# Row numbers kept as integers beside the rows, padding rows that name spare rows themselves, and no limiting operation per tile

## What is computed

```python
logits = x @ Wg + bg                                   # 8 experts
topk_vals, topk_idx = top_k(logits, 2)
topk_w = softmax(topk_vals)
h  = relu(x @ W1[e] + b1[e])                           # 256 -> 512, for each chosen expert e
eo = h @ W2[e] + b2[e]                                 # 512 -> 256
y  = x + sum over the 2 chosen experts of topk_w * eo
out = gamma * (y - mean(y)) * rsqrt(var(y) + 1e-5) + beta
```

## Time and profile before

| | us |
|---|---|
| median of 3 runs | 2370.67 (2370.27 to 2372.32) |
| profiled execution, its own time | 2372.47 |
| profiled execution, span of its instructions | 2370.8 |
| TensorE busy | 2167.7 (91%) |
| VectorE busy | 2049.7 (86%) |
| GpSimd busy | 1875.7 (79%) |
| ScalarE busy | 1661.8 (70%) |

### The profile page before, as it was taken

How to read it: one execution, slowest core, us unless ns; L and a number is a source line. 1 busy time by engine, 2 the same in 40 slices (tenths; PEclk the granted TensorE clock), 3 DMA queues, 4 the chain that set the end, 5 groups by cost and what they waited for, 6 DMA issues and landing times. The chain is left out here.

```text
span 2370.8 us, 47215 instructions
## 1 busy us (share of the span) xinstructions
PE 2167.7 (91%) x13383; PEld 1744.9 (74%) x13384; DVE 2049.7 (86%) x2983; ACT 1661.8 (70%) x3402; POOL 1875.7 (79%) x1176
## 2 busy tenths in 40 slices
PE   8889899999989898989899999999878999989995
PEld 5667677776767777767677777677677989979884
DVE  5899999999999999999999999999997556647775
ACT  6686878878787878776878877777774444436553
POOL 3787989898898989888889898988896566556563
PEclk9999999999999999999999999999998999999998
DMA  5041313223241404131314233231425667657674
GB/s 176 1 144 46 134 60 129 86 94 109 72 146 44 160 21 162 44 136 51 129 55 134 72 108 100 81 121 59 132 65 189 112 129 148 113 81 130 138 142 110
DMA packets 213919, 246.71 MB, mean 104 GB/s; under 512 B 96723, under 2 KB 178675, under 8 KB 213556
## 3 DMA queue, kind: packets, MB, share of 16 engines
q1 hardware_dynamic: 163092, 191.29, 26.2%
q0 software_dynamic: 29904, 34.77, 8.2%
q10 hardware_dynamic: 20688, 17.85, 2.5%
HBM read 180.50 MB, written 63.32 MB: 103 GB/s over the span
## 5 line engine op out<-in xcount | busy, mean ns | idle before, releaser
L878 POOL TENSOR_TENSOR dbu<-drive_u,w_all 128x1024 f32<-128x1024 f32 x384 | 904.2, 2363 | 102.0 <-DVE ps_a L742 49.2
L1157 ACT ACTIVATE ps_a<-delta,a_neg 128x512 f32<-128x512 f32 x768 | 517.3, 685 | 141.3 <-DVE area L742 124.8
L895 POOL TENSOR_TENSOR wp<-area 128x1024 f32<-128x1024 f32 x192 | 453.0, 2359 | 36.5 <-DVE area L742 35.8
L2024 POOL DMA_INDIRECT acc_scratch<-ow,idx x135 | 220.0, 1630 | 208.8 <-DMA acc_scratch<-ow,idx 127.4
L754 DVE TENSOR_TENSOR wd<-ps_a,area 128x1024 f32<-128x1024 f32 x320 | 383.9, 1200 | 0.0
L1421 PEld LDWEIGHTS ps_y<-ident,wd 128*128 128x128 f32 x2560 | 304.0, 145 | 97.3 <-issue 71.4
L1421 PE MATMUL ps_y<-ident,wd 128*128 128x128 f32 x2560 | 342.0, 279 | 10.7 <-DVE wd L754 10.5
L1448 PEld LDWEIGHTS ps_a<-dg,duT 128*128 128x128 f32 x2048 | 253.0, 199 | 66.6 <-issue 64.3
L1448 PE MATMUL ps_a<-dg,duT 128*128 128x128 f32 x2048 | 263.4, 284 | 38.2 <-ACT carry L1164 35.7
L2235 PEld LDWEIGHTS e_ps_h<-xT,w_tile 128*128 128x128 f32 x2160 | 261.7, 193 | 25.7 <-DVE xT L1913 14.0
L2235 PE MATMUL e_ps_h<-xT,w_tile 128*128 128x128 f32 x2160 | 266.5, 277 | 12.8 <-DVE xT L1913 8.1
(11 more groups left out here) (252 smaller groups left out, 3762.5 us busy)
## 6 DMA issues: line engine op xcount, KB each, us to landing
area<-b_scratch SPq DMA_DIRECT2D x128, 512.0 KB, 4.7
w_all<-b_scratch SPq DMA_DIRECT2D x96, 512.0 KB, 4.1
dg<-xs_scratch SPq DMA_DIRECT2D x540, 32.0 KB
area<-in_L_attn_x_dram SPq DMA_DIRECT2D x32, 512.0 KB, 5.0
x_scratch<-area SPq DMA_DIRECT2D x16, 512.0 KB, 2.9
acc_scratch<-area SPq DMA_DIRECT2D x16, 512.0 KB
area<-x_scratch ACTq DMA_DIRECT2D x32, 256.0 KB
ee<-acc_scratch SPq DMA_DIRECT2D x32, 256.0 KB, 3.3
```

The costliest lines, as they stand in the source:

```text
L878: pool.tensor_tensor(dbu[:, k % NBU], du[:, g % 2, :].unsqueeze(1).broadcast_to([P, 2, CH]), bb[:, row:row + 2, :], ALU.mult).then_inc(dbu ...
L895: pool.tensor_tensor(wp[:, s % 2], ss[:, s % 2], cc[:, rows, :], ALU.mult).then_inc(wp_done, 1)
L1157: act.activation(dst, dl[:, g, :], ACT.Exp, scale=a_neg[:, g, n:n + 1]).then_inc(exp_done, 1)
L2024: pool.indirect_dma_start(out=acc_dram, out_offset=bass.IndirectOffsetOnAxis(ap=idx[:, old, :], axis=0), in_=ow[:, old, :], in_offset=None ...
```

## The change

Row numbers are written into column 257 as integers: the two ScalarE copies write to the same bytes seen as int32. The padding buffer becomes `pads`, four copies (RING) of 128 rows, and its column 257 holds the integer numbers of spare rows, T*P + 128*k + p, written by GpSimd in the place of `aside`. `store_pad` and `tail_store` take the copies in turn. `idx`, `aside` and their semaphores go; the scatter takes its indices straight from column 1 of `meta[:, slot]`, seen as uint32. So that a slot of `meta` is not overwritten while its scatter may still read it, the load of tile s now waits for `t_out[slot]`, the landing of the scatter of tile s-4, where it waited for `o_weighed` and `idx_done`.

```diff
 row_meta (mamba_block), and "columns1" likewise
-                act.copy(stage[:, :, D + 1], idf[:, 0, q * NT:(q + 1) * NT]).then_inc(meta, 1)
+                act.copy(stage[:, :, D + 1].bitcast(I32), idf[:, 0, q * NT:(q + 1) * NT]).then_inc(meta, 1)
 moe_block
-        pad = sb("pad", [P, D + 2])
+        pads = sb("pads", [P, RING, D + 2])
-        aside = sb("aside", [P, RING])
-        idx = sb("idx", [P, RING, 1], U32)
 tail_store, store_pad
-                    sync.dma_start(xs_dram[r:r + P, :], pad[:]).then_inc(pad_out, 16)
+                    sync.dma_start(xs_dram[r:r + P, :], pads[:, j % RING]).then_inc(pad_out, 16)
-                    sync.dma_start(acc_dram[r:r + P, :], pad[:, 0:D]).then_inc(acc_out, 16)
+                    sync.dma_start(acc_dram[r:r + P, :], pads[:, 0, 0:D]).then_inc(acc_out, 16)
-                act.dma_start(xs_dram[bass.ds(end_row, P), :], pad[:]).then_inc(pad_out, 16)
+                act.dma_start(xs_dram[bass.ds(end_row, P), :], pads[:, e % RING]).then_inc(pad_out, 16)
 set_up (VectorE)
-                dve.memset(pad[:, 0:D + 1], 0.0).then_inc(pad_done, 1)
-                dve.memset(pad[:, D + 1:], NOWHERE).then_inc(pad_done, 1)
+                dve.memset(pads[:, :, 0:D + 1], 0.0).then_inc(pad_done, 1)
 tile_step (VectorE)
-                        dve.wait_ge(aside_done, 1)
...
-                    dve.tensor_scalar(idx[:, old, :], meta[:, old, 1:], aside[:, old:old + 1], None, ALU.min
-                                      ).then_inc(idx_done, 1)
 store_tile (GpSimd)
-                    wait_apart(pool, passed, [(o_weighed, 1, s, 1 - RING), (idx_done, 1, s, 1 - RING)])
+                    wait_apart(pool, passed, [(t_out[slot], 16 // RING, s, -(16 // RING) * slot)])
...
-                    wait_apart(pool, passed, [(o_weighed, 1, t, 1), (idx_done, 1, t, 1)])
+                    wait_apart(pool, passed, [(o_weighed, 1, t, 1)])
...
-                        out=acc_dram, out_offset=bass.IndirectOffsetOnAxis(ap=idx[:, old, :], axis=0),
+                        out=acc_dram, out_offset=bass.IndirectOffsetOnAxis(ap=meta[:, old, 1:].bitcast(U32), axis=0),
...
-            pool.iota(aside[:], pattern=[[P, RING]], base=T * P, channel_multiplier=1,
-                      allow_small_or_imprecise_dtypes=True).then_inc(aside_done, 1)
+            pool.iota(pads[:, :, D + 1].bitcast(I32), pattern=[[P, RING]], base=T * P, channel_multiplier=1
+                      ).then_inc(pad_done, 1)
```

More of the change, by code:

```diff
@@ L1561, in moe_block @@
     PADS = E + NTT - 2 * T
-    NOWHERE = 1e9
     LAST = NC - 1
@@ L1653, in moe_block @@
         landed_set = sem("landed_counts_set")
-        aside_done = sem("aside_done")
         order_done = sem("order_step")
@@ L1664, in moe_block @@
         o_weighed = sem("o_weighed")
-        idx_done = sem("idx_done")
         t_out = [sem(f"tile_stored{i}") for i in range(RING)]
@@ L2110, in tail_step @@
                     act.copy(stage[:, :, D], wt[:])
-                    ins = act.copy(stage[:, :, D + 1], idf[:, 0, LAST * NT:(LAST + 1) * NT])
+                    ins = act.copy(stage[:, :, D + 1].bitcast(I32), idf[:, 0, LAST * NT:(LAST + 1) * NT])
                 else:
```

## The result

The changed kernel takes 2378.77 us (median of 6 runs, 2375.61 to 2382.33), the kernel before beside it 2370.47 (6 runs, 2369.53 to 2372.48): a ratio of 1.0027, 95% interval 1.0016 to 1.0037 (the quotient of the two medians alone is 1.0035). It is slower: the whole interval lies above 1. Whether the loss exceeds the 0.2% that the forecast took as the bound this timing alone leaves open, since the interval begins at 1.0016. The forecast was 2376.2 in a range of 2369.5 to 2382.5. The same kernel was timed again beside the experiments, as `changed_again`: 2384.18 against 2375.85, ratio 1.0046 (1.0029 to 1.0063). So the change costs 0.3 to 0.5%, 6 to 11 us.

A forecast was written before the change was run, and what follows sets the result against it. From 2054 to 2356 us the scatter chain was taken as the bound, TensorE in the loop part. Added waits of 4.3 less 1.0 in the tail, plus 2.2 in the loop, gave +5.5 us: 2376.2, range 2369.5 to 2382.5.

The forecast's parts named there:

- What bounds the kernel: TensorE in the loop part; from 2054 to 2356 us the scatter chain, with VectorE's idx beside it.
- What the change takes away: VectorE's 135 limiting operations, 27.5 us in all, go; taken as 0, as does ow starting 0.12 us sooner after metadata.
- The 1.0 us taken off for shorter queue steps: GpSimd loses a semaphore wait ahead of the load, shortening 16 queue-set scatter steps by 0.06 us each: 1.0 us saved.
- The hop: Scatter bound by the landing two tiles back starts 2.13 us after it, not 1.42, as the load's issue comes between.
- The chained hop: Scatter bound by the landing one tile back still starts 0.78 us after it; the added wait costs 0 there.
- The count of places: After 2054 us, seven hops two back pay, 4.3 us, less 1.0 gives 3.3; those between 2182 and 2213 are swallowed.
- The loop part: Seven hops slipping in the hardware loop could cost 0 to 8 us; 2.2 taken, as x1 read bursts fix long landings.
- The total: Whole kernel: 3.3 in the tail plus 2.2 in the loop part, 5.5 us slower; span 2376.3, median 2376.2.
- The skill's rule: GpSimd DMA estimate: 2.3 us for the 128 KB scatter, so the moved wait costs nothing and the sum is -1.0 us.
- Hidden wait (A): Rival: loop bursts hide the wait and tail hops are partly covered, -1 to +3 us, 2369.7 to 2373.7; chance 0.26.
- The loop slips in full (B): Rival: short landings become long as scatters drift into the bursts, 3.3 + 8 = 11.3 us slower, 2382; chance 0.12.
- Faster through shorter descriptor making (C): Rival: without idx each chain hop is 0.13 us shorter, 5.6 us less 3.3 of added wait, 2368.4; chance 0.06.

The follow-up runs named there:

- meta_on_act: Changed kernel with all metadata loads issued by ScalarE's queue, one step later, not GpSimd's: 2373.59 us, ratio 0.9999 to the kernel before.
- eight_slots: Changed kernel with eight metadata slots from tile 57 on, so the load there waits only for the weighing of tile s-4: 2374.32 us, ratio 1.0008.
- act_tail: Changed kernel with the metadata loads of tiles 57 to 134 issued by ScalarE's queue, one step later: 2370.47 us, ratio 0.9971.
- before_act_tail: Kernel before, float numbers and limiting kept, with only the metadata loads of tiles 57 to 134 moved to ScalarE's queue: 2362.05 us, ratio 0.9958.
- copy_idx: Changed kernel, but VectorE copies the integer numbers from the metadata into idx and the load has its old waits: 2375.43 us, ratio 1.0012.
- wait_only: Kernel before, with only the metadata load's wait moved to the landing of the scatter of tile s-4: 2383.8 us, ratio 1.005.
- order_first: Kernel before, with only GpSimd's look into order read ahead of its wait for the landing two back: 2368.63 us, ratio 0.9982.
- the kernel before with the two edits: Kernel before with late metadata loads (tiles 57 to 134) on ScalarE's queue and order read ahead of the landing wait: 2356.8 us, ratio 0.9929.
- the changed kernel with them: Changed kernel with late metadata loads on ScalarE's queue, eight slots, and order read ahead of the landing wait: 2362.39 us, ratio 0.996.
- the pair without the early look: Late loads on ScalarE's queue: in the changed kernel with eight slots, 2364.44 us (0.9965); in the kernel before, 2362.05 us (0.9958).

## Why the prediction was right, and where it was not

- **What bounds the kernel: right.** Every experiment that moved the load or the look in GpSimd's queue moved the tail (in `meta_on_act` the loop part took the gain back); taking VectorE's limiting away, in `eight_slots`, did not shorten the time.
- **What the change takes away: right at 0.** `eight_slots` against the kernel before, and `act_tail` against `before_act_tail`, show it: with the wait's price gone or shared, the kernels with and without the limiting are level (1.0008, and 0.9971 beside 0.9958, with intervals that overlap). The 0.12 that I gave `ow` behind a landing of the metadata came, and went into slack: it starts 0.09 after the landing, where it was 0.24. What I did not see is that behind `ot` it starts later: 0.57 us after the start of `ot`, where it was 0.46 (and is 0.46 in `copy_idx`, which has a small operation there again), presumably since `idx` had covered VectorE's own wait for `ot`.
- **The 1.0 us taken off for shorter queue steps: wrong.** The wait did go from the queue, but two scatters that the queue alone spaces are 2.52 to 2.53 us apart at the least before and after. Nothing was saved there; why was not traced.
- **The hop: right in kind, a little long.** I wrote 1.42 + 0.70 = 2.13; it is 2.03 to 2.04. Of the 0.09 too much, 0.06 is the queue's wait at 2089.79 in the earlier trace rows with the issue behind it. I had counted it into the 0.70, though the change takes it away. From the queue step behind it to the load's start it is 0.64 before (2089.85 to 2090.49) and 0.64 after (2124.51 to 2125.15).
- **The chained hop: right.** It is 0.78 in all cases.
- **The count of places: wrong, and this is the step that failed.** I named seven places and had 3.3 us from them. The path through the changed tail has 13 hops two back, 2.03 on average, and so does `changed_again`. All of the path that is no landing grew by 8.2. Place by place, the seven that I named gave 3.6 of their 4.3 and no queue step gave back the 1.0. The rest came from places that I had left out: 2.7 at tiles 90, 93, 97 and 99, the others mostly between tiles 108 and 114. The places I called swallowed, "between 2182 and 2213", were not: there the scatters of tiles 90, 96, 97 and 99 started 1.43 after the landing two back, and that of tile 93 1.75, and I took the 1.4 to 2.1 us between `ow` and scatter for a bound by `ow`. After the change the first of them reads:

```profile
2174.59 3.83 DMA acc_scratch<-ow,e_meta
2178.42 0.02 issue
2178.44 0.05 POOLq L1995
...
2180.46 4.71 DMA acc_scratch<-ow,e_meta
```

  Its landing is at 2178.42 and the scatter starts 2.04 later, on the chain that ended last. For tiles 90 and 93 that was a plain misreading: their `ow` starts 4.0 and 4.5 us ahead of the scatter. For tile 96 it was 1.96 before and is 3.8 after, as the lag that is handed on has eaten the margin, and the hop came in full there too. Only at 97 and 99 was part of it swallowed (hops of 2.3, which is 2.5 behind the scatter before, with `ow` 2.8 and 1.8 us ahead), and even so each is 0.9 longer than it was. Tiles 110, 112 and 113 (2259.71, 2265.27 and 2268.20 before, with 1.49, 1.43 and 1.75) and tile 122 (2304.80, 1.43) were not on my list at all; after, 112 has 2.04. The tail's lag grows from -0.1 at tile 57 to 4.2 at 96, 7.6 at 112 and 10.1 at the end.
- **The loop part: wrong, about 0 in place of 2.2,** though 0 was the lower bound. From the landing of tile 26 to that of tile 56 it took 106.9 before and 106.5 after, 107.8 in `wait_only` and 108.9 in `changed_again`, but also 108.4 in `copy_idx`, which lacks the moved wait. So the kernels with and without it can't be told apart there, and 30 tiles at TensorE's 3.50 us are 105. The reason I gave stands only in part. The alternation of long and short landings, 5.32 and 5.51 in the earlier trace rows, was absent in the profiled execution after:

```profile
1999.91 3.64 DMA acc_scratch<-ow,e_meta
2006.84 3.34 DMA acc_scratch<-ow,e_meta
2014.02 3.94 DMA acc_scratch<-ow,e_meta
```

  (The 3.34 of the second ends at the first of the 16 counts of its landing; the last comes 3.82 after the start, so that one is short too.) The loop's landings took 4.48 on average before, 4.05 after, but 4.47 in `changed_again`, which is the same kernel, and 4.16 in `order_first`. So it is no property of the change. That it hangs on how the scatters fall against the x1 read was argued, not shown. Whichever it was, TensorE was not held: 700 matmuls in 102 us after, 699 in `changed_again`.
- **The total** of +5.5 was met at a span of +5.7 in part by offset: a tail of about 8 from the hops and 2 from landings that were longer on average (50 of them, 208.6 against 210.5 us), less the 4.2 that the same execution had gained ahead of tile 57. By the times, +8.3 in both timings, it was short by 3. That 5.5 came so near is luck: a tail three times as dear as I had it, no loss in the loop part where I had 2.2, and an execution that was ahead by 4.2 at tile 57.
- **The skill's rule.** By the Trainium skill, page DMA: Bandwidth & Descriptors, section Anatomy of one DMA — SWDGE (gpsimd) path, the landing should have been in before the load's turn. Counted to the last of its 16 counts, no scatter landed in less than 3.46 us before and 3.64 after; the wait was real, and the rows decided rightly.
- **The rivals.** Hidden wait (A): refuted by `wait_only`. The loop slips in full (B): did not happen. Faster through shorter descriptor making (C): did not happen, and it names the wrong operation. In the loop part the scatter's record on GpSimd did get shorter (GpSimd's groups of 1945 to 2047; instructions, busy time, mean ns):

```profile
L2015 POOL DMA_INDIRECT acc_scratch<-ow,e_meta x29 | 46.4, 1601 | 36.0 <-DMA acc_scratch<-ow,e_meta 27.0 <-issue 8.9
```

  It was 1725 in the earlier trace rows. But `wait_only`, with the limiting in place, has 1617, and `copy_idx`, which has a small operation there too and the old wait, 1714. So whether the small operation exists does not decide. The timelines of the kernel before show what does:

```profile
1998.28 0.69 DVE L1949 TENSOR_TENSOR area<-area,drive_u 128x512 f32 x1
1998.42 2.01 POOL L2024 DMA_INDIRECT acc_scratch<-ow,idx  x1 [1.63 <-DMA acc_scratch<-ow,idx]
...
2001.49 1.59 POOL L2024 DMA_INDIRECT acc_scratch<-ow,idx  x1 [0.44 <-issue]
```

  The first scatter starts while VectorE's addition of L1949 is running, and its record ends 1.46 us after that addition does. The second starts before the next such addition and takes 1.59. All nine records of 1.70 us and more in the loop part of the kernel before are of the first kind, and end 1.46 to 1.49 after the end of L1949; `idx` runs at the start of none of them. The changed kernel has no such long record there, because its scatters start at other times in VectorE's round. In the tail, where hops count, the mean was 1602 before and 1604 after: nothing to gain. The Trainium skill, page SBUF — State Buffer, section SBUF: two separate sides, says that GpSimd can't write descriptors while VectorE runs an operation in a 2-port mode. The rows agree in kind, as the record waits for the end of a VectorE operation; in which mode that one ran they do not show.

What stays open: why the kernel before with the two edits (2356.8) came out 5.6 us under the changed kernel with them (2362.39). They were timed beside different runs of the kernel before, but their ratios to these differ as well (0.9913 to 0.9945 against 0.9948 to 0.9972), so something in the changed kernel, its eight slots or ScalarE's wait for landings may still cost 0.3%. Their tails are level (291.3 and 290.7), though taken from an execution 5.0 over the median of the one and 4.6 under that of the other, and the pair without the early look, timed together, differs by 2.4 the same way with intervals that overlap. Also open is what makes a scatter land in 3.5 or 5.5 us: the average over the tail's 78 landings moved between 4.04 and 4.30 over the kernels, which is 13 us on a path with 50 of them, with no edit that explains it.

## What to carry to other kernels

When a wait is moved, look at what stands behind it in that engine's queue: no new event was awaited here, yet the load's issue of 0.6 us went from the time in which GpSimd waited anyway into the time after the landing, on a path with 12 such hops. When you count the places that a lag will hit, do it with the lag already in them: a hop whose margin is a microsecond is on the path once the lag is larger. And where an in-order queue sets a chain's pace, ask first what in it could go ahead of the wait or to another queue: a table look of 0.6 us and a 1 KB load, moved, made the kernel 0.7% faster, where 27.5 us of work taken from a busy engine beside the chain gave nothing.

## What the runs showed of the hardware that was not expected

- A small DMA costs its queue time whether anyone waits for it or not. On GpSimd two scatters are 2.53 us apart with a 1 KB load and its look-up between them and 1.85 without; on ScalarE its queue record is 0.34 us:

```profile
1989.99 0.34 ACTq L2056 DMA_DIRECT2D e_meta<-xs_scratch  x1
```

- Reading one word into a register for a wait's threshold, with the queue steps that come with it, cost GpSimd 0.6 us: the hop fell from 1.39 to 0.79 when it was read ahead. It is as dear as the issue of the load.
- A short operation taken out did not let the next one start sooner: with `idx` gone, `ow` starts 0.57 after the start of `ot`, not 0.46.
- 1 KB of metadata, 8 bytes for each of 128 rows, took 2.89 to 5.04 us to land in the chains that ended last, nearly as long as the 128 KB scatter beside it.
- The record of a scatter on GpSimd that starts while VectorE's addition of 128x512 (L1949) is running ends 1.46 to 1.49 us after the addition does, and so takes up to 2.10 us in place of 1.59.
